# Attention weights and values in single precision, one head in each slot

## Chip, cores and metric

The kernel runs on one core of a Trainium2 chip. The metric is the device time of one execution in microseconds (us), first to last instruction and what lies around it.

## What is computed

For x of 4 x 512 x 256 a transformer block in hyperbolic space is added to x, and then an LSTM over the 512 positions is added to that. The reference, cut to what matters here:

```python
xm = expmap0(xn * (1 + sc_msa) + sh_msa)
q = _to_heads(plin(xm, w_q, b_q))        # 16 heads of 16
k = _to_heads(plin(xm, w_k, b_k))
v = _to_heads(plin(xm, w_v, b_v))
qt, kt, vt = (logmap0(q), logmap0(k), logmap0(v))
scores = jnp.einsum('bhqd,bhkd->bhqk', qt, kt) / math.sqrt(HD)
attn = jax.nn.softmax(scores, axis=-1)
out_h = expmap0(jnp.einsum('bhqk,bhkd->bhqd', attn, vt))
...
def step(carry, xw_t):                   # 512 steps, one after the other
    prev_h, prev_c = carry
    a = xw_t + prev_h @ Wh
    i, f, o, g = sigmoid(a[:, 0:H]), sigmoid(a[:, H:2*H]), sigmoid(a[:, 2*H:3*H]), tanh(a[:, 3*H:])
    next_c = f * prev_c + i * g
    next_h = o * jnp.tanh(next_c)
    return ((next_h, next_c), next_h)
x = x + block(x)
x = x + lstm(x)
```

(The line with i, f, o and g stands for four lines of the reference.)

## The kernel before

**Stages.** The 512 positions are cut in four blocks of 128 (`NB`), for each of the 4 batch rows (`B`), so there are 16 tiles of 128 rows. A first loop over the 16 tiles makes q, k and v of all of them (0 to 244 us). Then come blocks j = 0 to 3: attention of the block's 4 tiles, then its projection, hidden layer and the input gates of the LSTM. The LSTM steps of block j-1 run inside block j: block 0 has no steps beside it, blocks 1 to 3 have 128 each, and the last 128 steps run alone at the end.

**Slots.** Every engine runs the same list of slots in program order (`along_attention`). In blocks 1 to 3 a slot begins with one LSTM step. Of the 128 slots of a block the first 68 hold attention: 16 for each tile (`PAIR_SLOTS`), shifted so that the multiplication with the values comes `LEAD` = 4 slots behind the scores. A pair of slots handles a head pair hp: the even slot q = 2hp makes the scores of key half 0, the odd one those of half 1. In slots 0 to 3 of a block nothing is multiplied with values, and in slots 64 to 67 no scores are made.

**TensorE** in a slot: the step (`pe_step`, L713: 32 matmuls, 128x8), the scores (`scores`, L594: two matmuls of 256 columns, for two heads and 128 keys each), and in even slots `weighted` of hp-2 (L609: for both heads and four key chunks, a high and a low half of the weights, so 16 fp16 matmuls of 33 columns: 16 high value columns, a column of ones for the sum, 16 low ones). `q_transposed` (L583) puts 8 small transposes in once in each tile. In the while loop over the first three tiles of a block the operands' addresses come from registers; the last tile's slots are written out with constant addresses.

**ScalarE** (`exps`, L833) makes the exponential of each half twice: once in single precision into `w32` (the tiles named tmp and fT in rows) and once in fp16 into `weights`. It waits for the scores, for the low half of two pairs ago, and in half 0 for `t_AV`, that is, until `weighted` of hp-2 is through.

**The low parts** (`low_weights`, L340): GpSimd subtracts the fp16 weights from the single-precision ones for half 0, VectorE for half 1. `weighted` waits for both (`t_l0`, `t_l1`).

**VectorE** takes the step's gates (L1255 to L1279; L1262 makes i*g, L1276 is the last one before the next step's matmuls), and divides by the sums in `normalize`. In the first loop GpSimd (L411, L414, L416) makes high and low values, scaled by `V_UP` (L1137).

The wait that orders ScalarE against TensorE:

```python
def exps(k, hp, half):
    n = HP * k + hp + 1
    if half == 0:
        act.wait_ge(s["t_AV"], n)
    act.wait_ge(s[f"t_l{half}"], n)
    act.wait_ge(s[f"t_S{half}"], n)
```

Of the kernel before, what the change touches and what calls it, by code (L numbers as in the profile page):

```python
# [80 lines left out]
def bass_hyperbolic_block_then_lstm(nc, x, cond, w_q, b_q, w_k, b_k, w_v, b_v, w_o, b_o, w_f1, b_f1, w_f2, b_f2,  # L81
                                    w_ada, b_ada, w_x, w_h, b_l, out):
    ctx = ExitStack()
    with ctx:
# [29 lines left out]
        vs = sb("vs", [P, B, NB, H, 2 * HD + 1], F16)  # L114
# [9 lines left out]
        weights = sb("weights", [P, 2, 2, NB, 2 * P], F16)  # L124
        wh = weights[:, :, :, :, :].rearrange("p a b c d -> p (a b c d)").bitcast(F32).rearrange("p (k n) -> p k n", k=KD)
# [251 lines left out]
        def _(pool):  # L377
# [26 lines left out]
            with pool.Fori(0, NT) as k:  # L404
# [4 lines left out]
                vh, vl = (vs[:, bass.ds(k % B, 1), bass.ds(k // B, 1), :, i * (HD + 1):i * (HD + 1) + HD].rearrange("p o r h e -> p (o r h) e")  # L409
                          for i in range(2))  # L410
# [101 lines left out]
        def _(pe):  # L512
# [86 lines left out]
            def weighted(k, b, hp):  # L599

                for half in range(2):
                    pe.wait_ge(s[f"t_l{half}"], HP * k + hp + 3)
                if hp % (HP // 2) == 0:
                    pe.wait_ge(s["t_o"], 2 * k + 1 + hp // (HP // 2))
                for e in range(2):
                    h = 2 * hp + e
                    for kc in range(NB):
                        for wl in range(2):
                            last = mm(sums(h), weights[:, hp % 2, wl, kc, e * P:(e + 1) * P], tile_of(vs, b)[:, kc, h, :],  # L609
                                      start=kc == 0 and wl == 0, stop=kc == NB - 1 and wl == 1, skip_group_check=True)  # L610
                last.then_inc(s["t_AV"], 1)

            def pe_attention(k, b, q):
# [762 lines left out]
```

## Time and profile before

| | |
|---|---|
| median of 3 runs | 1925.82 us (1925.07 to 1926.33) |
| profiled execution, span from first to last instruction | 1925.3 us |
| busy: TensorE matmul, VectorE, ScalarE, GpSimd | 1176.5, 1243.4, 1049.3, 403.0 us |
| mean granted TensorE clock, share of 2.4 GHz | 0.624 |

The span lies within 0.6 us of the median, so what is summed against the span holds for the runs too. Busy shares are averages over stages with different limits: no engine is full, and each stage has its own chain.

### The profile page before, as it was taken

The page shows a single profiled execution, that of the slowest core. Times are in us where ns is not written, and L with a number is a line of the kernel's source. Part 1 is how long each engine was busy: PE and PEld are TensorE (multiplying, and loading weights), DVE is VectorE, ACT ScalarE, POOL GpSimd, SP SyncE. Part 2 cuts the span into 40 slices and gives each one's busy share as a digit, 9 for nine tenths or more (in the row PEclk, how much of TensorE's full clock was granted, in tenths as well). Part 3 has the DMA queues.
Part 4 walks back from the last instruction along what each step waited for, and adds up shares of the span by engine and source line. Part 5 has one row for each costly group of instructions (what it writes and reads, how often), then busy time and mean ns, then how long its engine had stood idle before and what let it go on. Part 6 is the DMA issues. An engine that isn't in the chain of part 4 may idle for free.

```text
span 1925.3 us, 63564 instructions
## 1 busy us (share of the span) xinstructions
PE 1176.5 (61%) x20911; PEld 944.1 (49%) x20911; DVE 1243.4 (65%) x6652; ACT 1049.3 (55%) x4313; POOL 403.0 (21%) x802
## 2 busy tenths in 40 slices
PE   4666676186776448867664488667654875444444
PEld 4544444155555445655554466555544565333333
DVE  6466634223887776657887766588876665666666
ACT  0333388235777655657776556577765564444443
POOL 4222234422221132211111323112213130000000
PEclk9676655587555558965555689655555886555555
DMA  8000000000000000000000000000000000000000
GB/s 254 0 0 0 0 1 1 1 1 1 2 0 0 2 3 2 3 25 2 0 0 2 3 2 3 25 2 0 1 3 2 2 3 12 0 0 0 0 0 11
DMA packets 14555, 17.79 MB, mean 9 GB/s; under 512 B 3348, under 2 KB 13208, under 8 KB 14360
## 3 DMA queue, kind: packets, MB, share of 16 engines
q1 hardware_dynamic: 10248, 10.50, 1.7%
q10 hardware_dynamic: 4112, 4.86, 0.8%
q8 instruction: 102, 1.67, 0.4%
q14 instruction: 93, 0.76, 0.1%
HBM read 13.25 MB, written 2.10 MB: 8 GB/s over the span
## 4 chain that ended last, share of the span: by engine, by line
DVE 37%; PE 25%; ACT 16%; issue 12%; POOL 6%; DMA 1%; ACTq 1%; POOLq 1%; DVEq 0%; SPq 0%
PE psum L713 10%; DVE cnew L1266 6%; DVE cadd L1262 5%; DVE gA L1255 5%; ACT tC L963 4%; DVE gO L1259 3%; DVE h L1273 3%; PE psum L699 3%; DVE h L1276 3%; DVE gF L1257 3%; POOL sc L224 3%; PE psum L557 2%; ACT weights L833 2%; PE psum L667 2%; DVE h L1274 2%
## 5 line engine op out<-in xcount | busy, mean ns | idle before, releaser
L713 PE MATMUL psum<-h,wh 128*128 128x8 f16 x16384 | 515.7, 172 | 512.0 <-DVE h L1276 492.4
L713 PEld LDWEIGHTS psum<-h,wh 128*128 128x128 f16 x16384 | 475.1, 103 | 635.1 <-DVE h L1276 605.5
L957 ACT ACTIVATE tA<-gA 128x16 f32<-128x16 f32 x512 | 114.2, 223 | 372.7 <-DVE gA L1255 370.2
L1255 DVE TENSOR_TENSOR_SCAN gA<-coef,psum 128x48 f32<-128x48 f32 x512 | 129.4, 253 | 192.9 <-PE psum L713 192.3
L963 ACT ACTIVATE tC<-cnew 128x8 f32<-128x8 f32 x512 | 110.2, 215 | 163.3 <-DVE cnew L1266 151.0
L1262 DVE SCALAR_TENSOR_TENSOR cadd<-tA 128x8 f32<-128x8 f32 x512 | 140.8, 275 | 51.7 <-ACT tA L957 45.3
L594 PE MATMUL psum<-qbd,kT 128*128 128x256 f16 x512 | 152.3, 402 | 26.4 <-ACT weights L833 23.1
L1273 DVE TENSOR_TENSOR h<-oU,tC 128x8 f16<-128x8 f32 x512 | 87.6, 171 | 105.6 <-ACT tC L963 105.0
L833 ACT ACTIVATE weights<-psum 128x512 f16<-128x512 f32 x256 | 152.1, 594 | 0.0
L1266 DVE TENSOR_TENSOR_SCAN cnew<-cmul,cadd 128x32 f32<-128x32 f32 x512 | 128.2, 250 | 22.2
L340 POOL TENSOR_TENSOR weights<-tmp,weights 128x512 f16<-128x512 f32 x64 | 73.9, 1155 | 321.2 <-ACT weights L833 321.2
L609 PE MATMUL psum<-vs,weights 128*128 (+1 forms) x2048 | 128.1, 198 | 17.2 <-DVE weights L340 16.8
L609 PEld LDWEIGHTS psum<-vs,weights 128*128 128x128 f16 x2048 | 117.0, 110 | 39.5 <-issue 26.1
L340 POOL TENSOR_TENSOR weights<-fT,weights 128x512 f16<-128x512 f32 x64 | 74.3, 1161 | 242.0 <-ACT weights L833 242.0
L959 ACT ACTIVATE cmul<-gF 128x8 f32<-128x8 f32 x512 | 109.9, 215 | 0.0
L961 ACT ACTIVATE tO<-gO 128x8 f32<-128x8 f32 x512 | 107.6, 210 | 0.0
L1259 DVE TENSOR_TENSOR_SCAN gO<-coef,psum 128x24 f32<-128x24 f32 x512 | 102.7, 201 | 3.6
L1257 DVE TENSOR_TENSOR_SCAN gF<-coef,psum 128x24 f32<-128x24 f32 x512 | 102.4, 200 | 0.0
L1276 DVE TENSOR_TENSOR h<-h 128x8 f16<-128x8 f32 x512 | 87.7, 171 | 17.8
L952 ACT ACTIVATE psum<-arena 128x16 f32 (+1 forms) x513 | 96.1, 187 | 1.5 <-issue 1.2
L953 ACT ACTIVATE psum<-arena 128x16 f32 (+1 forms) x513 | 90.8, 177 | 0.6 <-issue 0.6
L224 POOL TENSOR_TENSOR sc<-sc,cst 128x2 f32<-128x2 f32 (+3 forms) x100 | 84.2, 842 | 19.5 <-POOL sc L272 10.4
(227 smaller groups left out, 2238.6 us busy)
## 6 DMA issues: line engine op xcount, KB each, us to landing
arena<-in_x_dram SPq DMA_DIRECT2D x4, 512.0 KB, 9.8
wf<-in_L_cond_w_f_dram SPq DMA_DIRECT2D x2, 1024.0 KB, 19.8
xs<-in_x_dram SPq DMA_DIRECT2D x4, 512.0 KB, 5.3
out_dram<-place SPq DMA_DIRECT2D x16, 128.0 KB, 1.9
arena<-in_L_cond_w_ada_dram ACTq DMA_DIRECT2D x1, 1536.0 KB
weights<-in_L_cond_Wh_dram ACTq DMA_DIRECT2D x1, 1024.0 KB, 14.3
gates<-in_L_cond_b_ada_dram ACTq DMA_DIRECT2D x8, 128.0 KB, 15.1
wx<-in_L_cond_Wx_dram SPq DMA_DIRECT2D x1, 1024.0 KB, 21.3
```

Of the source, the lines that this page charges most:

```text
L340: return engine.tensor_tensor(weights[:, buf, 1, kcs, :], w32[buf][:, half], weights[:, buf, 0, kcs, :], ALU.subtract)
L594: last = mm(bank[half][:, i * 2 * P:(i + 1) * 2 * P], tile_of(kT, b)[:, hp, kc * P:(kc + 1) * P], qbd[:, hp, :], start=True, stop=True, sk ...
L609: last = mm(sums(h), weights[:, hp % 2, wl, kc, e * P:(e + 1) * P], tile_of(vs, b)[:, kc, h, :], start=kc == 0 and wl == 0, stop=kc == NB ...
L713: last = mm(gate_cols(bk, gi, 1)[:, 0, :, 0:2], wh16[:, half, kc, (g0 + gi) * P:(g0 + gi + 1) * P], h16[:, kc, :, :], start=gi == 0 and kc ...
L833: last = A(dst.rearrange("p a b -> p (a b)"), bank[half], ACT.Exp, scale=1.0 / (math.sqrt(HD) * QK_UP * QK_UP))
L963: A(tC[:], cnew[:, :, 3], ACT.Tanh).then_inc(s["l_tC"], 1)
L1255: d.tensor_tensor_scan(gA[:], coef[:].rearrange("p c e -> p (c e)"), pA[:, 0:48], 0.0, ALU.mult, ALU.add).then_inc(s["l_gA"], 1)
L1257: d.tensor_tensor_scan(gF[:], coef[:, 0:8].rearrange("p c e -> p (c e)"), pF[:, 0:24], 0.0, ALU.mult, ALU.add).then_inc(s["l_gF"], 1)
L1259: d.tensor_tensor_scan(gO[:], coef[:, 0:8].rearrange("p c e -> p (c e)"), pO[:, 0:24], 0.0, ALU.mult, ALU.add).then_inc(s["l_gO"], 1)
L1262: d.scalar_tensor_tensor(cadd[:, :, 2], tA[:, 8:16], 1.0, tA[:, 0:8], ALU.add, ALU.mult).then_inc(s["l_ig"], 1)
L1266: d.tensor_tensor_scan(cnew[:].rearrange("p c e -> p (c e)"), cmul[:].rearrange("p c e -> p (c e)"), cadd[:].rearrange("p c e -> p (c e)") ...
L1276: d.tensor_tensor(lo, h32[:], hi, ALU.subtract).then_inc(s["l_lo"], 1)
```

## The change

The weights stay in single precision (`w32`), the values too (`vs` is now f32, 17 columns for a head: 16 values and the ones), and one single-precision matmul takes the place of two fp16 ones with 33 columns. The second exponential, `low_weights` on both engines, the making of high and low values and the scaling by `V_UP` go. `weighted` takes one head: the even slot has the first of the pair, the odd slot the second, and `t_AV` is given after the second. `normalize` loses a copy and an add. `wh` gets a buffer of its own.

```diff
-        vs = sb("vs", [P, B, NB, H, 2 * HD + 1], F16)
+        vs = sb("vs", [P, B, NB, H, HD + 1])
...
-        weights = sb("weights", [P, 2, 2, NB, 2 * P], F16)
...
-        def low_weights(engine, buf, half):
-
-            kcs = slice(half * NB // 2, (half + 1) * NB // 2)
-            return engine.tensor_tensor(weights[:, buf, 1, kcs, :], w32[buf][:, half], weights[:, buf, 0, kcs, :], ALU.subtract)
...
-                g.tensor_tensor(v32, lin[:, 2, :].rearrange("p (h e) -> p h e", e=HD),
+                g.tensor_tensor(v3, lin[:, 2, :].rearrange("p (h e) -> p h e", e=HD),
                                 num("f", 48)[:, 2 * H:3 * H].unsqueeze(2).to_broadcast([P, H, HD]), ALU.mult).then_inc(s["p_v"], 1)
-                hold(pool, "p_v", k + 2)
-                g.tensor_copy(vh, v32).then_inc(s["p_vh"], 1)
-                hold(pool, "p_vh", k + 1)
-                g.tensor_tensor(vl, v32, vh, ALU.subtract).then_inc(s["p_vl"], 1)
...
-                with pool.Fori(0, B * HP // 2) as i:
-                    for odd in range(2):
-                        hold(pool, "t_e0", B * HP * j + 2 * i + odd + 2)
-                        low_weights(g, odd, 0).then_inc(s["t_l0"], 1)
...
-            def weighted(k, b, hp):
-
-                for half in range(2):
-                    pe.wait_ge(s[f"t_l{half}"], HP * k + hp + 3)
...
+            def weighted(k, b, hp, e):
+
+                if e == 0:
+                    for half in range(2):
+                        pe.wait_ge(s[f"t_e{half}"], HP * k + hp + 2)
+                    if hp % (HP // 2) == 0:
+                        pe.wait_ge(s["t_o"], 2 * k + 1 + hp // (HP // 2))
+                h = 2 * hp + e
+                for kc in range(NB):
+                    last = mm(sums(h), w32[hp % 2][:, kc // (NB // 2), kc % (NB // 2), e * P:(e + 1) * P], tile_of(vs, b)[:, kc, h, :],
+                              start=kc == 0, stop=kc == NB - 1, skip_group_check=True)
+                if e == 1:
+                    last.then_inc(s["t_AV"], 1)
...
-                if q % 2 == 0 and hp >= 2:
-                    weighted(k, b, hp - 2)
+                if hp >= 2:
+                    weighted(k, b, hp - 2, q % 2)
...
-                act.wait_ge(s[f"t_l{half}"], n)
                 act.wait_ge(s[f"t_S{half}"], n)
-                for dst in (w32[hp % 2][:, half], weights[:, hp % 2, 0, half * NB // 2:(half + 1) * NB // 2, :]):
-                    last = A(dst.rearrange("p a b -> p (a b)"), bank[half], ACT.Exp, scale=1.0 / (math.sqrt(HD) * QK_UP * QK_UP))
-                last.then_inc(s[f"t_e{half}"], 1)
+                A(w32[hp % 2][:, half].rearrange("p a b -> p (a b)"), bank[half], ACT.Exp,
+                  scale=1.0 / (math.sqrt(HD) * QK_UP * QK_UP)).then_inc(s[f"t_e{half}"], 1)
...
-                d.tensor_scalar(num("f", 48)[:, 2 * H:3 * H], num("f", 48)[:, 2 * H:3 * H], V_UP, None, ALU.mult).then_inc(s["p_f"], 1)
...
-                if q % 2 == 1 and 1 <= q // 2 <= HP:
-                    hp = q // 2 - 1
-                    v.wait_ge(s["t_e1"], HP * k + hp + 2)
-                    low_weights(d, hp % 2, 1).then_inc(s["t_l1"], 1)
```

On TensorE, in a pair of slots of block 0's last tile (written out, no step in it), this stood before; L594 are the scores, L609 `weighted`, L583 the transposes of q:

```order
L594 MATMUL psum<-qbd,kT 128x256 [waits s_t_e0]
L594 MATMUL psum<-qbd,kT 128x256
L609 MATMUL psum<-vs,weights 128x33 [waits s_t_o,s_t_l1,s_t_l0]
L609 MATMUL psum<-vs,weights 128x33 x15
L594 MATMUL psum<-qbd,kT 128x256 [waits s_t_e1]
L594 MATMUL psum<-qbd,kT 128x256
L583 MATMUL psum<-ident,words 128x128 [waits s_t_q,s_t_qc]
L583 MATMUL psum<-ident,words 128x128 x7
L594 MATMUL psum<-qbd,kT 128x256 [waits s_t_e0]
```

At the same place the changed kernel has this (L574 are the scores, L588 `weighted`, L563 the transposes):

```order
L574 MATMUL psum<-qbd,kT 128x256 [waits s_t_e0]
L574 MATMUL psum<-qbd,kT 128x256
L588 MATMUL psum<-vs,tmp 128x17 [waits s_t_o,s_t_e1,s_t_e0]
L588 MATMUL psum<-vs,tmp 128x17 x3
L574 MATMUL psum<-qbd,kT 128x256 [waits s_t_e1]
L574 MATMUL psum<-qbd,kT 128x256
L588 MATMUL psum<-vs,tmp 128x17 x4
L563 MATMUL psum<-ident,words 128x128 [waits s_t_q,s_t_qc]
L563 MATMUL psum<-ident,words 128x128 x7
L574 MATMUL psum<-qbd,kT 128x256 [waits s_t_e0]
```

The second head's four matmuls now stand behind the odd slot's scores, right ahead of the scores that wait for `t_e0`.

On ScalarE, in the loop over the tiles of block 0, two head pairs were this before (L833 are the exponentials):

```order
L833 ACTIVATE tmp<-psum 128x512 [waits s_t_S0,s_t_l0,s_t_AV]
L833 ACTIVATE weights<-psum 128x512
L833 ACTIVATE tmp<-psum 128x512 [waits s_t_S1,s_t_l1]
L833 ACTIVATE weights<-psum 128x512
L829 REGISTER_ALU
L833 ACTIVATE fT<-psum 128x512 [waits s_t_S0,s_t_l0,s_t_AV]
L833 ACTIVATE weights<-psum 128x512
L833 ACTIVATE fT<-psum 128x512 [waits s_t_S1,s_t_l1]
```

and are this now (L811 are the exponentials):

```order
L811 ACTIVATE tmp<-psum 128x512 [waits s_t_S0,s_t_AV]
L811 ACTIVATE tmp<-psum 128x512 [waits s_t_S1]
L809 REGISTER_ALU
L811 ACTIVATE fT<-psum 128x512 [waits s_t_S0,s_t_AV]
L811 ACTIVATE fT<-psum 128x512 [waits s_t_S1]
```

Half of the exponentials are gone, and the one of half 0 still waits for `t_AV`, which now comes at the end of an odd slot.

## Rows read from the trace of the kernel before

**Rows 1.** The page's granted TensorE clock in 40 equal slices, tenths of 2.4 GHz.

```profile
PEclk9676655587555558965555689655555886555555
```

**Rows 2.** Windows: busy us of each engine (instructions), clock share, DMA; two stretches.

```profile
475.00:660.00 185.00, 125.16 (x2712) 100.91 (x2712) 148.64 (x772) 135.00 (x526) 35.92 (x31) 0.50 0.00 1
...
1620.00:1900.00 280.00, 118.25 (x3712) 107.86 (x3712) 184.74 (x1278) 119.84 (x698) 0.00 (x0) 0.50 0.00 0
```

**Rows 3.** Timeline, block 1, two slots: start us, length us, engine, line, [idle before].

```profile
479.97 0.85 PEld L583 LDWEIGHTS psum<-ident,words 128*128 128x128 f16 x8
...
481.16 1.02 PE L713 MATMUL psum<-h,wh 128*128 128x8 f16 x32
...
482.06 0.61 PE L594 MATMUL psum<-qbd,kT 128*128 128x256 f16 x2
...
482.09 1.16 POOL L340 TENSOR_TENSOR weights<-tmp,weights 128x512 f16<-128x512 f32 x1 [4.43 <-ACT weights L833]
...
482.33 0.94 DVE L1262 SCALAR_TENSOR_TENSOR cadd<-tA 128x8 f32<-128x8 f32 x1
...
482.45 1.16 PE L609 MATMUL psum<-vs,weights 128*128 x16
...
484.32 1.02 PE L713 MATMUL psum<-h,wh 128*128 128x8 f16 x32 [0.71 <-DVE h L1276]
...
486.73 1.02 PE L713 MATMUL psum<-h,wh 128*128 128x8 f16 x32 [0.95 <-DVE h L1276]
```

**Rows 4.** Timeline of TensorE, block 1: slots 4, 64 and 68 begin with L713.

```profile
475.58 1.02 PE L713 MATMUL psum<-h,wh 128*128 128x8 f16 x32 [0.95 <-DVE h L1276]
...
650.11 1.02 PE L713 MATMUL psum<-h,wh 128*128 128x8 f16 x32 [1.22 <-DVE h L1276]
650.98 0.61 PE L609 MATMUL psum<-vs,weights 128*128 128x33 f16 x16
...
660.51 1.02 PE L713 MATMUL psum<-h,wh 128*128 128x8 f16 x32 [1.40 <-DVE h L1276]
```

**Rows 5.** Timeline, block 0: its first exponential, a slot boundary, its last value matmuls.

```profile
246.67 0.60 ACT L833 ACTIVATE tmp<-psum 128x512 f32<-128x512 f32 x1
...
257.19 0.60 ACT L833 ACTIVATE tmp<-psum 128x512 f32<-128x512 f32 x1 [0.73 <-PE psum L609]
257.68 0.59 ACT L833 ACTIVATE weights<-psum 128x512 f16<-128x512 f32 x1
...
258.41 0.61 PE L594 MATMUL psum<-qbd,kT 128*128 128x256 f16 x2 [0.73 <-ACT weights L833]
...
331.98 0.62 PE L609 MATMUL psum<-vs,weights 128*128 128x33 f16 x16 [1.42 <-DVE weights L340]
```

**Rows 6.** Timeline of weight loads (PEld): single-precision matmuls; each leaves two records.

```profile
21.07 10.31 PEld L523 LDWEIGHTS psum<-c0T,arena 128*128 128x128 f32 x48 [7.82 <-DVE fT L1072]
...
55.20 4.17 PEld L568 LDWEIGHTS psum<-c0T,weights 128*128 128x128 f32 x32
...
1186.31 3.25 PEld L699 LDWEIGHTS psum<-uT,wx 128*128 128x128 f32 x16
...
1190.37 1.86 PEld L699 LDWEIGHTS psum<-uT,wx 128*128 128x128 f32 x16
```

**Rows 7.** One line's instructions: ns min/median/max.

```profile
L523 PE MATMUL psum<-c0T,arena x48: 354/354/374, 21.1 to 31.1; 128*128 128x4 f32 x48
```

**Rows 8.** Windows as in rows 2: during L523, and behind L568.

```profile
22.00:24.00 2.00, 2.00 (x11) 2.00 (x11) 1.97 (x2) 0.00 (x0) 1.83 (x1) 1.00 1.01 194
...
59.00:60.00 1.00, 0.88 (x7) 0.49 (x6) 0.41 (x3) 0.00 (x0) 0.00 (x0) 0.72 0.00 0
```

**Rows 9.** Groups by line in 60:244: busy us, mean ns | idle before, releaser.

```profile
L1153 DVE COPY words<-words 128x256 f16<-128x256 f16 x16 | 10.5, 654 | 0.0
...
L576 PEld LDWEIGHTS psum<-ident,words 128*128 128x128 f16 x128 | 9.0, 108 | 10.1 <-DVE words L1155 9.4
...
L1155 DVE COPY words<-words 128x256 f16<-128x256 f16 x16 | 3.9, 244 | 0.0
```

More of the change, by code:

```diff
@@ L123, in bass_hyperbolic_block_then_lstm @@
         xin = flat[:, KD * 6 * D:KD * 6 * D + (NT + 1) * D].rearrange("p (t d) -> p t d", d=D)
-        weights = sb("weights", [P, 2, 2, NB, 2 * P], F16)
-        wh = weights[:, :, :, :, :].rearrange("p a b c d -> p (a b c d)").bitcast(F32).rearrange("p (k n) -> p k n", k=KD)
+        wh = sb("wh", [P, KD, 4 * D])[:, :, :]
         place = sb("place", [P, 4 * B * D])
@@ L408, in _ @@
                 hold(pool, "p_f", k + 1)
-                vh, vl = (vs[:, bass.ds(k % B, 1), bass.ds(k // B, 1), :, i * (HD + 1):i * (HD + 1) + HD].rearrange("p o r h e -> p (o r h) e")
-                          for i in range(2))
-                g.tensor_tensor(v32, lin[:, 2, :].rearrange("p (h e) -> p h e", e=HD),
+                v3 = vs[:, bass.ds(k % B, 1), bass.ds(k // B, 1), :, 0:HD].rearrange("p o r h e -> p (o r h) e")
+                g.tensor_tensor(v3, lin[:, 2, :].rearrange("p (h e) -> p h e", e=HD),
                                 num("f", 48)[:, 2 * H:3 * H].unsqueeze(2).to_broadcast([P, H, HD]), ALU.mult).then_inc(s["p_v"], 1)
-                hold(pool, "p_v", k + 2)
-                g.tensor_copy(vh, v32).then_inc(s["p_vh"], 1)
-                hold(pool, "p_vh", k + 1)
-                g.tensor_tensor(vl, v32, vh, ALU.subtract).then_inc(s["p_vl"], 1)
                 ch.full()
@@ L597, in scores @@
                 last.then_inc(s[f"t_S{half}"], 1)
-            def weighted(k, b, hp):
-                for half in range(2):
-                    pe.wait_ge(s[f"t_l{half}"], HP * k + hp + 3)
[L603 to L611, printed above, removed]
+            def weighted(k, b, hp, e):
[10 more added lines that the diff above has]
+                    last.then_inc(s["t_AV"], 1)
             def pe_attention(k, b, q):
@@ L729, in _ @@
             pe.wait_ge(s["p_kc"], NT + 1)
[L730 removed]
+            pe.wait_ge(s["p_v"], NT + 1)
             pe.wait_ge(s["l_init"], 2)
@@ L1134, in _ @@
                                            REACH, num("ct", 3)[:, i:i + 1], ALU.mult, ALU.min)
-                last.then_inc(s["p_fq"], 1)
-                v.wait_ge(s["p_fq"], n)
-                d.tensor_scalar(num("f", 48)[:, 2 * H:3 * H], num("f", 48)[:, 2 * H:3 * H], V_UP, None, ALU.mult).then_inc(s["p_f"], 1)
+                last.then_inc(s["p_f"], 1)
                 v.wait_ge(s["p_f"], n)
@@ L1185, in normalize @@
                 heads = slice(half * H // 2, (half + 1) * H // 2)
-                three = sums(half * H // 2, H // 2).rearrange("p (h e) -> p h e", e=2 * HD + 1)
+                three = sums(half * H // 2, H // 2).rearrange("p (h e) -> p h e", e=HD + 1)
                 o3 = (o4[:, b] if isinstance(b, int) else o4[:, bass.ds(b, 1), :].rearrange("p o d -> p (o d)")).rearrange("p (h e) -> p h e", e=HD)
                 v.wait_ge(s["t_AV"], HP * k + (half + 1) * HP // 2 + 2)
-                d.reciprocal(num("rd", H)[:, heads], three[:, :, HD])
-                d.tensor_copy(vlow[:, heads, :], three[:, :, HD + 1:]).then_inc(s["t_r"], 1)
+                d.reciprocal(num("rd", H)[:, heads], three[:, :, HD]).then_inc(s["t_r"], 1)
                 v.wait_ge(s["t_r"], 2 * k + half + 1)
-                d.tensor_tensor(vlow[:, heads, :], three[:, :, 0:HD], vlow[:, heads, :], ALU.add).then_inc(s["t_r2"], 1)
-                v.wait_ge(s["t_r2"], 2 * k + half + 1)
-                d.tensor_tensor(o3[:, heads, :], vlow[:, heads, :], num("rd", H)[:, heads].unsqueeze(2).to_broadcast([P, H // 2, HD]),
+                d.tensor_tensor(o3[:, heads, :], three[:, :, 0:HD], num("rd", H)[:, heads].unsqueeze(2).to_broadcast([P, H // 2, HD]),
                                 ALU.mult).then_inc(s["t_o"], 1)
```

14 lines of the change are left out of this document (4 added, 10 removed).

## Prediction

> **What bounds the kernel now.** I read the windows by stage first, then the timeline of two neighbouring slots, then the same without an LSTM step. The clock line and the windows show that TensorE runs at half clock (1.2 GHz) in the attention of blocks 1 to 3 and in the lone steps [rows 1, 2]. No engine is full there: of 185 us TensorE is busy 125, VectorE 149, ScalarE 135, GpSimd 36 [rows 2].
>
> The timeline shows what does bound a slot [rows 3]. Steps begin at 481.16, 484.32 and 486.73: an even slot takes 3.16 us, an odd one 2.41, a pair 5.57. Each begins when VectorE's L1276 has made the new h, so the chain of the step sets the pace, and TensorE waits for it 0.71 and 0.95 us. The 0.75 us by which the even slot is longer is one row: L1262 takes 0.94 us there, while GpSimd's L340 is running (482.09 to 483.25). In the odd slot GpSimd has nothing and the 0.75 is not there; so I take it as a wait for GpSimd's operation. Slots 4 to 63 last 650.11 - 475.58 = 174.5 us, the last four 10.4 [rows 4]; blocks 2 and 3 repeat them.
>
> In block 0 there is no step. There ScalarE starts an exponential as soon as `weighted` has ended, TensorE waits for two of them and begins the next scores 0.14 us after the second (257.68 + 0.59 to 258.41) [rows 5]. TensorE and ScalarE take turns.
>
> **The change part by part.** *What goes.* The low weights on GpSimd and the second exponential: 1.16 us of GpSimd, 1.2 us of ScalarE and a subtraction of VectorE for each head pair. With them goes the 0.75 us at L1262, so the step's chain would allow 2.41 us in every slot, 4.82 in a pair, against 5.57 now. This is the gain, if TensorE lets it through.
>
> *What TensorE gets.* No row before has a single-precision matmul with 17 columns. The nearest are L523 with 4 columns and L699 with 128. Each such matmul leaves two records. L523: 48 loads in 10.31 us, that is (10.31 - 0.33) / 47 = 0.213 us a record [rows 6] (0.33 for the last load itself, its median length). L699 at half clock, 128 columns: 3.25 / 16 = 0.203 [rows 6]. So between 4 and 128 columns the price hardly moves: it is the load of the weights that costs, and the columns go beside it. I take 0.213; 0.203 is the lower end. One head is 4 matmuls, 8 records, 8 x 0.213 = 1.70 us; a pair 3.41, against 1.16 for the 16 fp16 matmuls [rows 3]. That is 2.25 us more for each pair, and there is 0.71 + 0.95 us of waiting to hide it in.
>
> *A slot of blocks 1 to 3.* In program order: step, from L713 to the next matmul 0.90 (481.16 to 482.06) or 0.87 (650.11 to 650.98), I take 0.88, scores 0.39 to `weighted` (482.45; I take 0.40) [rows 3, 4], then the head 1.70. Sum 2.98, a pair 5.96. It is over the chain's 4.82 and over today's 5.57: TensorE becomes the bound, without a gap. The exponential that waits for `t_AV` at the end of the odd slot lasts 0.60 and lies beside the next step's 0.88; its cover is just enough. Were it gone, TensorE would wait as in block 0 below. The step's gates come 0.6 us before they are needed. Thirty pairs: 178.8. The transposes of q (0.85 us [rows 3]) were in the waiting and now add up: four in a block, 3.4. So slots 4 to 63 take 182.2 against 174.5: +7.7. Slots 0 to 3 lose one 0.75. Slots 64 to 67 take 4 x (0.88 + 1.70) = 10.3 against 10.4. Each block +6.9, three blocks **+20.6**.
>
> *Block 0.* A pair on TensorE is scores 0.40 + head 1.70, then scores 0.40 + head. The second head has to be complete: 7 x 0.213 + 0.354 (a matmul's own length [rows 7]) = 1.85. Only then does the exponential of half 0 start (0.04), take 0.60, and release the next scores 0.14 later [rows 5]: 0.78 us without cover, since there is no step, except once in a tile, where the transposes of q lie in it. A pair is 0.40 + 1.70 + 0.40 + 1.85 + 0.78 = 5.13. The first exponential starts at 246.67; with one in place of two the scores of slot 4 start at about 248.8 (two rounds of 0.60 + 0.14 with scores between). Thirty pairs, 153.9, end at 402.7; four heads and the last one's end 6.9, at 409.6. Before, the last value matmul ended at 331.98 + 0.62 = 332.6 [rows 5]. Block 0: **+77**. ScalarE, which was the fuller one here, has half the work; nothing comes of it, since TensorE does not wait for its amount but for its place.
>
> *First loop.* GpSimd's L414 and L416 go. VectorE's L1153 takes 654 ns beside L416, its twin L1155, alone, 244 [rows 9]. L1151 stands beside L414 in the same way, and L1137 goes. That is 0.4 us in a round from L1153 alone, with the others perhaps twice that (an estimate); but TensorE's transposes wait for VectorE only 9.4 us over the 16 rounds [rows 9], behind that stand the q, k and v matmuls. Bounds 0 and 9.4; I take **-6**.
>
> *The rest.* `normalize` loses two short VectorE operations; in blocks 1 to 3 they lie beside the 0.6 us of slack, at the end of block 0 they give perhaps 0.5 (an estimate from the 0.2 to 0.6 that such short operations take here). The buffer of `wh`, the removed waits and the smaller values cost nothing. Hidden layer, gates and the lone steps have no edit.
>
> Sum: 77 + 20.6 - 6 - 0.5 = +91 on a span of 1925.3, so 2016.5; the median stood 0.5 above the span: 2017.
>
> **The clock.** All this is at half clock. L523 ran ten us without a gap and held 0.213 a record to the end; L699 shows the two paces, 0.203 at half and 1.86 / 16 = 0.116 at full clock [rows 6]. The window there shows 1.00 [rows 8], which its pace contradicts, it being that of L699 at half clock; I go by the pace. L568, nearly the work that is added (4 columns), came behind matmuls with many more columns and ran faster (4.17 / 32 = 0.130 a record [rows 6]); it kept TensorE busy without a gap, and the clock fell as it ended (0.72 in 59 to 60 us [rows 8]). So TensorE without gaps, on weight loads, has not raised the clock in this trace.
>
> The Trainium skill says otherwise on its face: TensorE: Matmul & The Clock Gate, Part 1, has it that the default is throttled and that activity releases the throttle. By that rule a TensorE without gaps in blocks 1 to 3 would go to full clock, and it would be the first rival below. L523 speaks against reading "activity" as busy records.
>
> **The rivals.** *Full clock, faster.* If it rises in attention, a head costs 8 x 0.116 = 0.93. In blocks 1 to 3 TensorE then needs at most 0.88 + 0.40 + 0.93 = 2.21, less than 2.41, and the chain is free of L1262's wait: 60 x 2.41 = 144.6 against 174.5, with the ends -31.4 in each block, -94 in all. Block 0, the 512 columns of scores in half of 0.40: pair 0.20 + 0.93 + 0.20 + 1.05 + 0.78 = 3.16, end near 347, +15. With -6: 1841. It decides from about half of the attention at full clock. For it: TensorE has no gaps any more. Against: L523, L568, and that the streams of columns do not get denser. 8%.
>
> *Address price, slower still.* In the loop over three tiles the addresses come from registers: 16 fp16 value matmuls take 1.16 us there [rows 3] and 0.61 where they are constant [rows 4], 0.034 a record more. If the single-precision ones pay it on top of their load, 192 heads x 8 x 0.034 = +52: 2069. Against it: a record of 0.213 leaves 0.15 us in which such work can lie. 9%.
>
> *No change.* The 2.25 us hidden by today's waiting of 1.66 and the 0.75 that VectorE gets back. The sum of a slot says no for blocks 1 to 3 by 0.4 us a pair only, but block 0 has no such gap. 2%.
>
> **How the numbers follow.** My forecast has 81%, 2017, by its own bounds (0.203 a record: -21; first loop 0 or 9.4) 1992 to 2025. The 80% range takes in the address price's end: 1990 to 2068. A measurement of this kernel tells about 0.2% from no change. Faster 0.08, same 0.02, slower 0.90.
>
> **What would show it.** In the changed profile: steps in pairs of 5.96 us in blocks 1 to 3, evenly 2.98, with TensorE's idle before L713 gone; 8 records of a head in 1.70; clock 0.50; L1262 without its 0.94; GpSimd idle in attention; the last value matmul of block 0 near 410 us; a wait of 0.78 for ScalarE there before every other scores. Wrong would be: a clock near 1.0 in the windows of attention, slots of 2.41, or a record of a head at 0.24 and above.

## The result

| | before | after |
|---|---|---|
| median | 1926.07 us (1925.07 to 1928.8, 4 runs) | 1969.48 us (1968.54 to 1972.14, 4 runs) |
| profiled span | 1925.3 us | 1966.8 us |
| mean granted TensorE clock | 0.624 | 0.63 |

The changed kernel is slower: the ratio is 1.0225, 95% interval 1.021 to 1.0239. I had forecast 2017, with 1990 to 2068 as range: the sign was right, the size was twice what came (+91 forecast, +43 measured, +41.5 between the spans), and the time lies outside the range.

The page of the changed kernel: busy time of each engine, and the clock in 40 slices, against [rows 1].

```profile
PE 1414.9 (72%) x20911; PEld 1253.1 (64%) x20911; DVE 1063.4 (54%) x6444; ACT 938.9 (48%) x4057; POOL 235.5 (12%) x642
...
PEclk9778755569655565985555669755556797555555
```

TensorE has 238 us more than before, VectorE 180 less. Its windows, in the columns of [rows 2]: first loop, then slots 4 to 63 of block 1.

```profile
60.00:225.00 165.00, 97.11 (x425) 76.06 (x426) 93.08 (x333) 61.87 (x129) 28.98 (x64) 0.78 0.00 0
...
518.00:695.00 177.00, 176.80 (x2551) 170.03 (x2551) 100.98 (x685) 102.68 (x434) 0.00 (x0) 0.50 0.00 1
```

In attention TensorE is busy 176.8 of 177 us and yet at the lower of its two levels, 1.2 GHz. Its timeline, in the order of time: the first scores; a slot boundary of the tile loop in block 0; a tile boundary; pairs of the last tile; the end of block 0's attention; the first step; slot 6 of block 1 and the start of slot 7; its slot 64 and the start of slot 65. The bracket is the idle time before the row.

```profile
224.68 0.61 PE L574 MATMUL psum<-qbd,kT 128*128 128x256 f16 x4 [1.36 <-ACT qbd L802]
...
325.24 1.89 PE L588 MATMUL psum<-vs,tmp 128*128 x8
326.96 0.59 PE L574 MATMUL psum<-qbd,kT 128*128 128x256 f16 x2
...
333.87 1.87 PE L588 MATMUL psum<-vs,tmp 128*128 x8
...
342.27 0.61 PE L574 MATMUL psum<-qbd,kT 128*128 128x256 f16 x2 [0.26 <-DVE place L1163]
...
356.64 0.61 PE L574 MATMUL psum<-qbd,kT 128*128 128x256 f16 x2 [0.69 <-ACT tmp L811]
357.04 1.73 PE L588 MATMUL psum<-vs,fT 128*128 128x17 f32 x8
358.61 0.59 PE L574 MATMUL psum<-qbd,kT 128*128 128x256 f16 x2
...
361.40 0.61 PE L574 MATMUL psum<-qbd,kT 128*128 128x256 f16 x2 [0.69 <-ACT fT L811]
...
373.50 3.58 PE L588 MATMUL psum<-vs,fT 128*128 128x17 f32 x16
...
508.61 0.94 PE L693 MATMUL psum<-h,wh 128*128 128x8 f16 x32 [1.98 <-ACT psum L931]
...
524.77 1.04 PE L693 MATMUL psum<-h,wh 128*128 128x8 f16 x32
...
526.05 1.73 PE L588 MATMUL psum<-vs,fT 128*128 x8
527.61 1.00 PE L693 MATMUL psum<-h,wh 128*128 128x8 f16 x32
...
695.34 1.00 PE L693 MATMUL psum<-h,wh 128*128 128x8 f16 x32
696.19 1.87 PE L588 MATMUL psum<-vs,tmp 128*128 128x17 f32 x8
697.90 1.00 PE L693 MATMUL psum<-h,wh 128*128 128x8 f16 x32
```

What the reader is to see: in block 0 every other scores row waits for ScalarE, except around a tile boundary (333.87 to 342.27). In slots 4 to 64 of block 1 the steps have no bracket any more, except at slot 4: step, scores, head and the next step join. From its start to the start of what follows, a head takes 1.57 us behind scores (357.04 to 358.61, 526.05 to 527.61) and 1.71 behind the step (696.19 to 697.90). In the tile loop, where addresses come from registers, nearly every first head of a pair takes 1.68 to 1.73 behind scores too (325.24 to 326.96); the one of slot 6 in block 1 (526.05) does not.

Cut by stage, from the two timelines (first scores, end of the last value matmul of block 0, first step, the step behind block 3):

| stage | before | after | difference | forecast |
|---|---|---|---|---|
| start to the first scores | 244.2 | 224.7 | -19.5 | -6 |
| attention of block 0 | 88.4 | 152.4 | +64.0 | +77 |
| rest of block 0 | 132.6 | 131.5 | -1.1 | -0.5 |
| blocks 1 to 3 | 1145.7 | 1143.8 | -1.9 | +20.6 |
| lone steps, end | 314.4 | 314.4 | 0 | 0 |

So the loss is block 0 alone, and a third of it is given back by the first loop.

### The profile page after: what moved, and what is told of

Same layout as the page of the kernel before. It is cut to its first block, busy times and chain, and to the rows that moved or that the text cites. A ratio compares the mean times of both kernels' runs of the same rounds, so it can differ in the third digit from the quotient of the medians.

```text
span 1966.8 us, 62266 instructions
## 1 busy us (share of the span) xinstructions
PE 1414.9 (72%) x20911; PEld 1253.1 (64%) x20911; DVE 1063.4 (54%) x6444; ACT 938.9 (48%) x4057; POOL 235.5 (12%) x642
## 4 chain that ended last, share of the span: by engine, by line
PE 56%; DVE 19%; ACT 9%; issue 8%; POOL 6%; DMA 1%; POOLq 1%; ACTq 1%; SPq 0%; DVEq 0%
PE psum L588 21%; PE psum L693 15%; PE psum L574 6%; PE psum L537 4%; PE psum L679 3%; DVE cnew L1235 3%; DVE gA L1224 3%; ACT tC L941 3%; POOL sc L220 2%; DVE h L1242 2%; DVE gO L1228 2%; PE psum L647 2%; DVE h L1245 2%; DVE gF L1226 1%; DVE cadd L1231 1%
## 5 line engine op out<-in xcount | busy, mean ns | idle before, releaser
L693 PEld LDWEIGHTS psum<-h,wh 128*128 128x128 f16 x16384 | 508.6, 104 | 423.0 <-DVE h L1245 389.3
L588 PEld LDWEIGHTS psum<-vs,tmp 128*128 128x128 f32 x1024 | 231.1, 331 | 11.5 <-issue 6.3
L588 PEld LDWEIGHTS psum<-vs,fT 128*128 128x128 f32 x1024 | 231.6, 331 | 8.3 <-issue 0.5
L588 PE MATMUL psum<-vs,tmp 128*128 (+1 forms) x1024 | 230.0, 366 | 0.0
L588 PE MATMUL psum<-vs,fT 128*128 (+1 forms) x1024 | 227.8, 364 | 0.0
L574 PE MATMUL psum<-qbd,kT 128*128 128x256 f16 x512 | 151.0, 398 | 17.4 <-ACT tmp L811 8.6
L941 ACT ACTIVATE tC<-cnew 128x8 f32<-128x8 f32 x512 | 110.2, 215 | 93.9 <-DVE cnew L1235 68.3
L1235 DVE TENSOR_TENSOR_SCAN cnew<-cmul,cadd 128x32 f32<-128x32 f32 x512 | 116.4, 227 | 24.3
L811 ACT ACTIVATE fT<-psum 128x512 f32<-128x512 f32 x128 | 74.6, 592 | 88.7 <-PE psum L588 88.1
L811 ACT ACTIVATE tmp<-psum 128x512 f32<-128x512 f32 x128 | 74.3, 591 | 85.3 <-PE psum L588 85.0
L1231 DVE SCALAR_TENSOR_TENSOR cadd<-tA 128x8 f32<-128x8 f32 x512 | 88.4, 173 | 45.5 <-ACT tA L935 42.1
L930 ACT ACTIVATE psum<-arena 128x16 f32 (+1 forms) x513 | 96.1, 187 | 0.3 <-DVE arena L1315 0.3
```

The source lines that it names most:

```text
L574: last = mm(bank[half][:, i * 2 * P:(i + 1) * 2 * P], tile_of(kT, b)[:, hp, kc * P:(kc + 1) * P], qbd[:, hp, :], start=True, stop=True, sk ...
L588: last = mm(sums(h), w32[hp % 2][:, kc // (NB // 2), kc % (NB // 2), e * P:(e + 1) * P], tile_of(vs, b)[:, kc, h, :], start=kc == 0, stop= ...
L693: last = mm(gate_cols(bk, gi, 1)[:, 0, :, 0:2], wh16[:, half, kc, (g0 + gi) * P:(g0 + gi + 1) * P], h16[:, kc, :, :], start=gi == 0 and kc ...
L811: A(w32[hp % 2][:, half].rearrange("p a b -> p (a b)"), bank[half], ACT.Exp, scale=1.0 / (math.sqrt(HD) * QK_UP * QK_UP)).then_inc(s[f"t_e ...
L941: A(tC[:], cnew[:, :, 3], ACT.Tanh).then_inc(s["l_tC"], 1)
L1235: d.tensor_tensor_scan(cnew[:].rearrange("p c e -> p (c e)"), cmul[:].rearrange("p c e -> p (c e)"), cadd[:].rearrange("p c e -> p (c e)") ...
```

## The experiments

Ten kernels in three groups, each group beside runs of the kernel before on the same chip, with medians of 1924.37 (experiments 1, 3, 4, 5; another chip than the rest), 1924.63 (6, 8, 9, 10) and 1927.61 us (2, 7). Ratios are against those; spans serve for the sums. The theory (A): the added work is the 8 weight loads of a head, at the pace of the 1.2 GHz level, and GpSimd's operations had cost VectorE in every stage. The rivals are named in the expectations.

**1. GpSimd's work of the first loop put back.** To the changed kernel were added a tile `back`, written and not read, and

```diff
+                hold(pool, "p_v", k + 2)
+                g.tensor_copy(back[:, 0], v3).then_inc(s["p_vh"], 1)
+                hold(pool, "p_vh", k + 1)
+                g.tensor_tensor(back[:, 1], v3, back[:, 0], ALU.subtract).then_inc(s["p_vl"], 1)
+                hold(pool, "p_vl", k + 1)
```

> The changed kernel, with two GpSimd operations put back behind the making of the values in the first loop (a copy to fp16 and a subtraction, as long as the removed ones, into a tile that nobody reads); the attention is untouched. If the first loop got 19.5 us shorter because GpSimd no longer held VectorE up (and because shorter rounds left TensorE at a higher clock), most of it comes back: 14 to 18 us more than the changed kernel, 1983 to 1987, with rounds of 11.3 us and a clock near 0.7 in the loop. If it was the removed VectorE scaling and the one shorter GpSimd operation that remains, it stays within 4 us of the changed kernel, 1969 to 1973.

Measured: 1982.77, ratio 1.0299 (1.0275 to 1.0324), span 1981.3, +14.5 on the changed kernel. The first scores start at 236.21 in place of 224.68: 11.5 of the 14.5 come back in the first loop itself, where a round is now 11.0 us on average and the clock 0.73 in 60 to 225 us. Another 2.7 lie in slots 68 to 127 of blocks 1 to 3, which this edit does not touch, and are variation between kernels. Groups of 60 to 225 us, in the changed kernel:

```profile
L537 PE MATMUL psum<-place,uT 128*128 128x256 f32 x192 | 71.8, 550 | 0.0
...
L1124 DVE CAST qhl<-place 128x256 f32 x16 | 4.7, 294 | 3.4 <-DVE place L1116 3.4
...
L1129 DVE COPY words<-words 128x256 f16<-128x256 f16 x16 | 3.4, 214 | 0.0
```

In the kernel before the CAST was this; L1129 was L1153 of [rows 9], 654 ns:

```profile
L1148 DVE CAST qhl<-place 128x256 f32 x14 | 10.3, 735 | 2.9 <-DVE place L1140 2.9
```

With GpSimd's work back the same CAST (L1130 there) stays short:

```profile
L1130 DVE CAST qhl<-place 128x256 f32 x15 | 4.4, 294 | 3.2 <-DVE place L1122 3.2
```

And the timeline of one round:

```profile
110.48 0.73 POOL L407 TENSOR_TENSOR back<-vs,back 128x256 f16<-128x256 f16 x1 [0.19 <-POOL back L405]
110.49 0.21 DVE L1135 COPY words<-words 128x256 f16<-128x256 f16 x1
...
110.63 0.67 DVE L1137 COPY words<-words 128x256 f16<-128x256 f16 x1
```

The two copies are alike. The one that runs beside L407 takes 0.67, the other 0.21. That is a wait like the one of [rows 9], made by putting GpSimd's operation back; it falls on the other twin (L1137, that is L1155 of before), since the rounds are placed otherwise. The Trainium skill (SBUF — State Buffer, Who interferes with whom) has it that a copy or a cast on VectorE can run in a mode that uses the pair of ports shared with GpSimd, and that whoever issues first holds the pair for the whole instruction; the 0.67 beside L407's 0.73 agrees. The 441 ns of the CAST did not come back, so they were not the doing of the two operations that went: before, it ran beside L411 (110.50 and 110.46 us), and in the changed kernel it starts 0.2 ahead of GpSimd's remaining operation (106.20 and 106.40). So it seems to be the timing of the two that moved.

**2. The same with VectorE's scaling of the factors too** (by 1.0, where before it was by `V_UP`):

```diff
-                last.then_inc(s["p_f"], 1)
+                last.then_inc(s["p_fq"], 1)
+                v.wait_ge(s["p_fq"], n)
+                d.tensor_scalar(num("f", 48)[:, 2 * H:3 * H], num("f", 48)[:, 2 * H:3 * H], 1.0, None, ALU.mult).then_inc(s["p_f"], 1)
```

> The changed kernel with GpSimd's two operations of the first loop back (into a tile that nobody reads) and also VectorE's scaling of the values' factors, by 1.0. GpSimd's operations alone gave 1982.8 and moved the first scores from 224.7 to 236.2 us, of 244.2 before the change. Theory A: the scaling and its place in VectorE's chain are the rest; 16 x 0.21 is 3.4 us for the operation itself, so 1985 to 1989, first scores at 239 to 243. Rival B: the scaling lies in waiting and costs nothing: 1981 to 1984, first scores at 236 to 237, and the rest is GpSimd's different load (it wrote narrower values before).

Measured: 1988.79, ratio 1.0315 (1.0298 to 1.0332), as theory A had it. First scores at 242.25, which is 6.0 later than in experiment 1, or 0.38 us a round. The operation itself is 0.175 of that; the six conversions behind it take 2.85 us together in place of 2.73, because other ones of them now fall beside GpSimd (the CAST is 388 ns, in 60 to 225 us). The rest is the operation's place in VectorE's chain, which is argued, not shown. Of the 19.5 us of the first loop, 11.5 are GpSimd's two operations, 6.0 the scaling with this shift, 1.9 stay open.

**3. Both heads in the even slot** (`t_AV` comes half a slot earlier, and the head pair is one lump of 16 records):

```diff
-                if hp >= 2:
-                    weighted(k, b, hp - 2, q % 2)
+                if q % 2 == 0 and hp >= 2:
+                    for e in range(2):
+                        weighted(k, b, hp - 2, e)
```

> The changed kernel, with both heads of a pair in the even slot, as before the change, in single precision. If a slot is bound by the longer of TensorE's program order and the step's chain, each slot by itself, the even slots of blocks 1 to 3 take 0.87 + 0.39 + 3.1 = 4.4 us and the odd ones 2.41: a pair 6.8 against 5.8, 90 us more, less 5 to 8 in block 0 where the odd slot's scores come to lie beside the exponential: about 2050. If only TensorE's total work counted, nothing would change: 1969, with 8 less for block 0.

Measured: 2073.03, ratio 1.0765 (1.0736 to 1.0794). Its timeline of TensorE in block 1:

```profile
529.12 1.02 PE L694 MATMUL psum<-h,wh 128*128 128x8 f16 x32 [0.95 <-DVE h L1246]
...
530.38 3.44 PE L588 MATMUL psum<-vs,tmp 128*128 x16
533.65 1.00 PE L694 MATMUL psum<-h,wh 128*128 128x8 f16 x32
...
536.04 1.02 PE L694 MATMUL psum<-h,wh 128*128 128x8 f16 x32 [0.95 <-DVE h L1246]
```

The next step has to stand behind the lump: the even slot is 4.53 (529.12 to 533.65), the odd one is back at the chain's 2.39 with TensorE idle for 0.95. Slots 4 to 63 take 209.1 in place of 177.2. One head a slot is what lets the weight loads use the waiting. In block 0 only 2.6 us were won, less than I expected, and the whole is 23 above the expected 2050: a pair is 6.92 in place of 6.8, and slots 64 to 67, which the expectation left out, take 13.4 in place of 10.2.

**4. The head ahead of the scores** (the wait for the exponential then has the scores as its cover):

```diff
-                if hp < HP:
-                    scores(k, b, hp, q % 2)
                 if hp >= 2:
                     weighted(k, b, hp - 2, q % 2)
+                if hp < HP:
+                    scores(k, b, hp, q % 2)
```

> The changed kernel, with the head's matmuls ahead of the scores in each slot. If block 0 pays 0.78 us in about 20 pairs because the exponential that waits for t_AV stands between the second head and the next scores, this puts the scores and the next head beside it: 16 us less in block 0 with pairs of 3.9 us; in blocks 1 to 3 the even slots lose the 0.2 us by which they are longer than the odd ones, 5 to 12 us together: 1941 to 1948. If TensorE is bound by the amount of weight loads alone, it stays at 1966 to 1970.

Measured: 1966.15, ratio 1.0214 (1.019 to 1.0238), hardly other than the changed kernel; two large effects cancel, 20.6 won in block 0 and 18.2 lost in blocks 1 to 3. Block 0's attention is 131.8 in place of 152.4, pairs of 3.9 without a wait. But slots 4 to 63 of a block take 182.6 in place of 177.2:

```profile
530.95 1.04 PE L693 MATMUL psum<-h,wh 128*128 128x8 f16 x32
531.85 1.87 PE L588 MATMUL psum<-vs,fT 128*128 x8
533.55 0.59 PE L574 MATMUL psum<-qbd,kT 128*128 128x256 f16 x2
533.94 1.04 PE L693 MATMUL psum<-h,wh 128*128 128x8 f16 x32
```

A slot is 2.99 (530.95 to 533.94), and the head 1.70 of it (531.85 to 533.55), where behind the scores it was 1.57. This is the slot that I had forecast, 2.98, and here it is, in the other order. The weight loads show why. The first two rows are of the changed kernel, in its last tile and in its tile loop, the third is of this kernel:

```profile
356.83 1.83 PEld L588 LDWEIGHTS psum<-vs,fT 128*128 128x128 f32 x8
...
325.23 1.78 PEld L588 LDWEIGHTS psum<-vs,tmp 128*128 128x128 f32 x8 [0.22 <-issue]
...
531.82 1.78 PEld L588 LDWEIGHTS psum<-vs,fT 128*128 128x128 f32 x8
```

Behind scores the first load starts 0.21 ahead of the head's first matmul (356.83, 357.04), beside the scores' stream of 256 columns; behind the step it starts 0.03 ahead (531.82, 531.85). The tile loop's first head starts its load only 0.01 ahead (325.23, 325.24), which is why it is as long as one behind the step. I had not expected this loss.

**5. 128 columns in each value matmul.** `vs` gets 111 more columns at its end, and the operands become

```diff
-                    last = mm(sums(h), w32[hp % 2][:, kc // (NB // 2), kc % (NB // 2), e * P:(e + 1) * P], tile_of(vs, b)[:, kc, h, :],
+                    last = mm(wide_sums(h), w32[hp % 2][:, kc // (NB // 2), kc % (NB // 2), e * P:(e + 1) * P], wide_values(b, kc, h),
```

(128 columns from the head's first one on; what lies beyond its 17 is overwritten by the next head or not read.)

> The changed kernel, but each value matmul takes 128 columns in place of 17: the head's own and 111 more that follow in memory; their sums are overwritten by the next heads or never read. The number of weight loads is the same. If a record's price is the load and the columns lie beside it (0.203 us with 128 columns at half clock before the change), the amount costs nothing at half clock. Theory A: what raises TensorE's clock is streamed columns, not loads; then the clock goes to 1.0 in attention, a head costs 0.93 us, slots of blocks 1 to 3 fall to the chain's 2.41 (30 us less in each block) and block 0's pairs to about 3.1 (55 us less): 1815 to 1835. Theory B: the clock does not follow the columns in this mixture and stays 0.50: 1969 to 1990, with slots of 2.8 to 3.1 as now.

Measured: 1826.38, ratio 0.9478 (0.9453 to 0.9504). Windows in block 0 and in block 1:

```profile
240.00:280.00 40.00, 33.40 (x267) 29.39 (x267) 1.99 (x8) 17.01 (x32) 0.00 (x0) 1.00 0.00 0
470.00:610.00 140.00, 125.82 (x2479) 112.36 (x2477) 96.29 (x658) 97.56 (x420) 0.00 (x0) 0.99 0.01 1
```

and its timeline of TensorE:

```profile
470.98 2.01 PE L600 MATMUL psum<-vs,tmp 128*128 x8
472.78 1.05 PE L705 MATMUL psum<-h,wh 128*128 128x8 f16 x32
...
484.80 0.96 PE L705 MATMUL psum<-h,wh 128*128 128x8 f16 x32 [0.28 <-DVE h L1258]
...
485.83 1.06 PE L600 MATMUL psum<-vs,fT 128*128 x8
487.16 0.96 PE L705 MATMUL psum<-h,wh 128*128 128x8 f16 x32 [0.27 <-DVE h L1258]
```

The same count of instructions, with 7.5 times the columns, is faster: the clock goes to 2.4 GHz, a head lasts 1.06 in place of 1.73 (length of its records), and the slot is 2.36, set by VectorE's h once more. TensorE is *less* busy (125.8 of 140 us) than in the changed kernel, where it was busy 176.8 of 177 at 0.50. The first head of the block, still at the lower level (clock 0.50 from 471 to 473 us), shows what 128 columns cost there: 1.80 (470.98 to 472.78), 0.09 more than with 17 at the same place (1.71, 519.45 to 521.16 in the changed kernel).

**6. The two together** (experiment 5 with the order of 4).

> The widened kernel (128 columns for each value matmul), with the head ahead of the scores in each slot. At half clock this order saved 20.6 us in block 0 and cost 6 us in each of blocks 1 to 3, since a head behind the step can't hide its first load. At full clock blocks 1 to 3 are bound by the step's chain, so if TensorE's length there is hidden the order costs nothing in them, and block 0 still loses its waits of 0.78 us: 15 to 20 us less, 1806 to 1811. If the order costs the same at full clock in blocks 1 to 3, half of 6 us each comes back: 1815 to 1820. If the clock falls, because the slots' mixture differs, it goes back towards 1960.

Measured: 1804.77, ratio 0.9364 (0.9346 to 0.9382), the fastest kernel that keeps single precision, 6.4% below the kernel before. Block 0's attention is 81.2; at the higher clock the order costs blocks 1 to 3 nothing (1050.8 us together, 1051.8 in experiment 5). The head itself is still longer behind the step, 0.97 (462.33 to 463.30) against 0.89 behind scores in block 0 of experiment 5, but TensorE waits for VectorE's h at the end of the slot and the 0.08 lies in that wait. The window of block 1:

```profile
448.00:594.00 146.00, 133.80 (x2549) 117.72 (x2550) 99.40 (x680) 99.60 (x432) 0.00 (x0) 0.97 0.01 2
```

**7. The same columns in the kernel before** (128 in place of 33, half precision, high and low parts):

> The kernel before, half-precision high and low parts, with 128 columns instead of 33 in each matmul with the values (the extra columns are never read). Theory A: in blocks 1 to 3 the chain of the step with the wait beside GpSimd sets the pace, not TensorE, so a higher clock gives little there: slots 4 to 63 stay at 168 to 176 us, and the time is 1900 to 1935. Then what the wide single-precision kernels gained came from both, the lighter VectorE and the clock. Rival B: the clock alone made that gain: slots of 2.4 us, slots 4 to 63 near 145, 1850 or less. Rival C: TensorE has gaps here, so the clock stays at half; 16 x 128 columns then last 1.71 us in place of 1.16: block 0 longer by 10 to 20 us, 1935 to 1960.

Measured: 1935.85, ratio 1.0047 (1.0032 to 1.0063). B is out. By the number it lies between A and C, but not where C put it: block 0's attention is 91.0 (before 88.4), where the clock is 0.98:

```profile
250.00:330.00 80.00, 56.21 (x622) 40.66 (x622) 33.33 (x63) 67.27 (x131) 33.91 (x30) 0.98 0.00 1
500.00:550.00 50.00, 39.34 (x728) 32.58 (x729) 39.74 (x204) 36.09 (x141) 10.45 (x9) 0.60 0.01 1
```

In block 1 the clock comes and goes (0.60). Its timeline of TensorE there:

```profile
483.14 0.96 PE L725 MATMUL psum<-h,wh 128*128 128x8 f16 x32 [0.40 <-DVE h L1289]
...
484.43 1.23 PE L621 MATMUL psum<-vs,weights 128*128 x16
486.31 0.96 PE L725 MATMUL psum<-h,wh 128*128 128x8 f16 x32 [0.65 <-DVE h L1289]
...
488.67 0.99 PE L725 MATMUL psum<-h,wh 128*128 128x8 f16 x32 [1.12 <-DVE h L1289]
```

Even where the matmuls run at the faster pace (the granted clock is 1.00 from 483 to 489 us) the pair lasts 5.53 (483.14 to 488.67), since both steps wait for VectorE's h. Slots 4 to 63 take 175.5, before 174.5. So in this kernel the higher clock is worth nothing in a pair while VectorE waits for GpSimd. That experiment 5 comes out below the kernel before takes both, the clock and the absence of that wait.

**8. The kernel before, both low parts on VectorE** (GpSimd's loop over `low_weights` goes):

```diff
+                if q % 2 == 0 and 1 <= q // 2 <= HP:
+                    hp = q // 2 - 1
+                    v.wait_ge(s["t_e0"], HP * k + hp + 2)
+                    low_weights(d, hp % 2, 0).then_inc(s["t_l0"], 1)
```

> The kernel before, with both halves of the low weights on VectorE and none on GpSimd. If L1262's 0.94 us is a wait for GpSimd's subtraction, the even slots fall from 3.16 to about 2.41 (VectorE's second subtraction of 0.69 us lies beside the step's matmuls, as the first does): 21 to 24 us less in each of blocks 1 to 3, 1852 to 1865. If it has another cause, VectorE only gets more work: 1926 to 1945.

Measured: 1872.53, ratio 0.9727 (0.9711 to 0.9743), a miss of 7.5 us above what I expected. The operation i*g over slots of block 1, first this kernel:

```profile
L1261 DVE SCALAR_TENSOR_TENSOR cadd<-tA 128x8 f32<-128x8 f32 x64 | 11.0, 172 | 3.9 <-ACT tA L952 2.5
```

then the kernel before:

```profile
L1262 DVE SCALAR_TENSOR_TENSOR cadd<-tA 128x8 f32<-128x8 f32 x60 | 26.1, 435 | 3.4 <-ACT tA L957 2.4
```

435 ns on average with GpSimd beside it, 172 without, though VectorE now makes the low parts of both halves. It is 0.94 in 19 of the 60 slots only; elsewhere the wait falls on a neighbour (L1266 280 ns on average against 225, L340 on tmp 876 against 687), and all of it comes to some 22 us. Slots 4 to 63: 158.0 against 174.5. Only 16.5 are won, since VectorE's second subtraction is not hidden everywhere: many slots are 2.41, others 2.5 to 3.4. So GpSimd's help with the low parts was a loss of 2.7%, and this edit alone would have beaten the change by 97 us.

**9. The kernel before, one head a slot** (its `weighted` cut as in the change, half precision as before).

> The kernel before, high and low half-precision parts as they were, but with one head in each slot. This is the placing part of the change alone. In blocks 1 to 3 TensorE needs 0.87 + 0.39 + 0.6 us in a slot, under the chain's 2.41, so nothing moves there; in block 0 the exponentials of half 0 start one head later and nothing hides them: 0 to 12 us more, 1925 to 1937. If the later t_AV delayed ScalarE in blocks 1 to 3 as well, up to 0.6 us in each pair would be added, 60 us.

Measured: 1937.57, ratio 1.006 (1.0043 to 1.0076). Blocks 1 to 3 are as before; block 0's attention is 100.3 in place of 88.4. TensorE's wait for ScalarE there, 0.73 in [rows 5]:

```profile
305.14 0.60 PE L594 MATMUL psum<-qbd,kT 128*128 128x256 f16 x2 [1.26 <-ACT weights L834]
```

So the later `t_AV` by itself costs block 0 11.9 us while ScalarE still makes two exponentials. That 11.9 of the +64 are this is not shown: in the changed kernel, experiment 3 gave `t_AV` early again and block 0 won 2.6.

**10. Half precision alone, in the changed kernel.** `vs` and the weights in half precision, with no low parts: this kernel leaves out the low parts of weights and values.

```diff
-        vs = sb("vs", [P, B, NB, H, HD + 1])
+        vs = sb("vs", [P, B, NB, H, HD + 1], F16)
...
-        w32 = [t.rearrange("p (a b c) -> p a b c", a=2, b=NB // 2)
+        w32 = [t.bitcast(F16)[:, 0:FF].rearrange("p (a b c) -> p a b c", a=2, b=NB // 2)
```

> The changed kernel, with weights and values in half precision and no low parts: the low parts are left out of the sum. Same slots, same waits, same ScalarE work; only the value matmuls' loads get short (one record of 0.03 to 0.07 us in place of two of 0.2). If the loads of single-precision weights are all that the change costs on TensorE, blocks 1 to 3 go to 2.41 us a slot (32 us less each) and block 0's pairs to 2.0 to 2.3 us (75 to 85 us less): 1785 to 1800. If the waits for t_AV and the one head per slot cost by themselves, block 0 stays over 100 us and the total over 1820.

Measured: 1796.93, ratio 0.933 (0.9314 to 0.9345). Its windows, blocks 0 and 1:

```profile
226.00:300.00 74.00, 54.99 (x406) 38.88 (x405) 4.89 (x20) 45.30 (x82) 0.00 (x0) 0.51 0.00 1
440.00:590.00 150.00, 102.12 (x2356) 84.48 (x2355) 102.84 (x702) 104.79 (x448) 0.00 (x0) 0.50 0.01 1
```

At the same clock, 0.50, and in the same order, block 0's attention is 74.8 in place of 152.4, slots 4 to 63 are 146.1 in place of 177.2. The 170.8 us between the spans of this kernel and the changed one are 77.6 there and three times 31.1 here: the single-precision loads of the 256 heads. Without them block 0 would be 13.6 shorter than before the change (88.4). The wide kernels win most of it back by the clock.

## Why the forecast was wrong

Point by point, by the steps of the prediction.

*The chain and L1262.* Right. L1231 (the L1262 of before) takes 170 ns in the changed kernel, and experiment 8 shows the same gain alone.

*The clock.* Right: 0.50 with TensorE busy 176.8 of 177. The rule that I had weighed (the Trainium skill, TensorE: Matmul & The Clock Gate, Part 1: the default is throttled and activity releases the throttle) does not hold if busy time is taken for activity. Experiment 5 changed only the number of columns, and there the granted clock is 0.99 with TensorE busy 125.8 of 140 us.

*A record of weights, 0.213 us.* Right where nothing with many columns stands before: 1.71 for eight (696.19 to 697.90), 2.56 for a slot without scores (forecast 2.58). Mis-sized as a constant: behind the scores a head is 1.57. This is the term that failed in blocks 1 to 3. Most slots were 2.80 to 3.02 in place of 2.98, so slots 4 to 63 took 177.2 in place of 182.2: 5.0 in each block, 15 in all. Experiment 4 shows it: with the order turned round nearly every slot without transposes is 2.98 or 2.99 and the 60 slots take 182.6. I had [rows 6] only, where loads stand behind loads.

*Blocks 1 to 3, the rest.* Slots 68 to 127 were forecast as unchanged and took 2.0 to 2.6 us less in each block, 7.1 in all. In slot 68 the shorter `normalize` still lies in VectorE's way, which I had put into the slack: 3.47 before (660.51 to 663.98), 3.19 after (705.58 to 708.77), 0.8 of the 7.1. The other slots have no edit, and their cause stays open. It goes with the change and not with the experiments' parts: these 180 slots take 552.7 to 556.6 us in the changed kernel and all that were made from it, and 559.4 to 562.4 in the kernel before and all that were made from it. So the precision, the split into slots, the columns, GpSimd's low parts and its work in the first loop are not the cause, and some 3 or 4 us between two kernels of one kind are variation.

*Block 0.* The wait's size was right: 0.69 in the last tile, 0.77 or 0.78 in the loop, forecast 0.78. The step that failed is that I gave it and the full 1.85 to all 30 pairs. Slots 4 to 63 took 140.8 (229.29 to 370.09) against 153.9. At each of the three tile boundaries the code gives a slot its old tile's head *ahead of* the next tile's scores, and no wait stands there: two pairs in 8.4 (333.87 to 342.27) in place of 10.26, 5.6 in all. The other 24 pairs took 4.82 on average in place of 5.13, again by the load that is hidden (4.76 from 356.64 to 361.40). The first stood in the order of the instructions, which I had read at one place only; the second stood in no row that I had. Experiment 10 shows that the loads make more than the whole +64: 77.6, with 13.6 won by the rest of the change.

*First loop.* The bound of 9.4 was wrong, and with it the range. I had taken it from the time that TensorE waited for VectorE in one row, and so left out that an operation in VectorE's chain also moves everything that is fed by it in the next round, and the operation L1137, which I let go for nothing and which is worth 6.0 with what it shifts. The prediction saw L1153 (654 to 214 ns) and took L1151 for a second one of the kind, but that hardly moved (651 to 616 ns); the largest was L1148, 735 to 294, and experiment 1 shows that GpSimd's two operations had not made it. A round of the loop took 11.5 us before and takes 10.0 to 10.8 now, 10.2 on average. The clock in 60 to 225 us went from 0.68 to 0.78 by the tighter rounds, and the projections' mean from 600 to 550 ns; how much of the 19.5 goes through the clock was not tested apart.

Sum: 13.0 in block 0, 22.5 in blocks 1 to 3, 13.5 in the first loop and 0.6 elsewhere are the 49.6 by which the forecast was too high. Every error had one sign: the loads and waits were taken at their unhidden end, and the gain of the first loop was bounded too low. (The upper end of my own bounds, 2025, is 2023 by its terms.)

The rivals: *full clock* did not come in the changed kernel, and experiments 5 and 6 show what it would do: forecast at 1841, measured 1826 where it was brought about. By stages experiment 5 is 14.9 above the kernel before in block 0 (forecast 15), 93.9 below in blocks 1 to 3 (forecast 94) and 17.9 below up to the first scores (forecast 6); the first loop is nearly the whole miss. *Address price*: forecast as 0.27 on every head of the tile loop (8 x 0.034), measured as 0.11 to 0.16 on most first heads of a pair (1.68 to 1.73 against 1.57) and nothing on the second. The load rows in experiment 4 show it as a first load that is not hidden and not as a price on each record; that register addresses are its cause was not tested apart.

## What to carry to other kernels

A single-precision weight load cost nearly the same here for 4, 17 and 128 columns (0.213, 1.71 / 8 = 0.214 and 0.203 us a record at 1.2 GHz, the first by its pace), and the first of a head hid behind 256 columns (1.57) and not behind 8 (1.71): price it by what stands directly ahead of it, and read the whole order, the boundaries of loops too. Time that one engine waits inside an operation for another counts as busy; look for twins of one operation with different lengths (0.94 and 0.17, 0.67 and 0.21). The slower twin can name a helper that costs more than it helps, as in experiment 8. Bound the gain of a shorter chain by the round, not by one engine's wait in it.

## What the hardware showed that I had not expected

TensorE at 1.2 GHz for 177 us with 0.2 us of idle, and at 2.4 GHz in the same program with more columns and 14 us of idle in 140 us. Columns that nobody reads took 143 us off the changed kernel (1969.5 to 1826.4). And at the lower clock a stream of 256 columns ahead of a load is worth 0.13 us, enough for the order of two calls to move 60 slots by 5.4 us; at the higher clock it is worth 0.08, and the kernel loses nothing by it, since VectorE sets the slot.
